# A four-layer residual LoRA kernel: the activation laid out batch by batch on chip, and one weight's split moved to GpSimd

## The chip, the core and the metric

The kernel runs on one core of a Trainium2 chip. The metric is device microseconds (us) of one execution; the kernel before takes 321.08 us (median of 3 runs, 320.62 to 321.49). TensorE (PE) multiplies, VectorE (DVE), ScalarE (ACT) and GpSimd (POOL) work element by element, and SyncE (SP) and ACT issue transfers, each on a queue of its own; the two queues are served by the same 16 DMA engines.

## The reference

`x` is [8 batches, 128 tokens, 512 features], fp32. Four residual layers follow each other, each with weights picked by one id per batch:

```
x = x + x @ w0[id0[b]].T                                  # layer 0: a whole 512x512 matrix per batch
x = x + x @ W.T + 2 * sum_e gate_e * (x @ A_e.T) @ B_e.T  # layer 1: router logits x @ Wr.T + 5*onehot(id1), top 2 of 8
x = x + x @ W.T + bias + 0.5 * (x @ A[id2[b]]) @ B.T      # layer 2
g, u = x@Wg.T + 0.5*lora_g, x@Wu.T + 0.5*lora_u           # layer 3, adapters by id3[b], inner size 1376
x = x + down(silu(g) * u) + 0.5*lora_d
```

## The kernel before, in words

The features lie on the 128 partitions in C = 4 chunks, and tokens run along the free dimension: `x_f` is a [128, 4, 1024] tile (chunk, then token; token = batch * 128 + position). Host code lays `x` out in DRAM as [batch][partition][chunk][token], so that one batch has 2 KB in a row per partition in DRAM.

The products want fp32 accuracy from a fast format (fp32r). So an operand is split into a high part (a copy that rounds to fp32r, `high`, on ACT, line 406) and a low part (the difference, `low`, on DVE, line 592), and a product is three matmuls: high x high, high x low, low x high. The activation of layer 0 is split on POOL instead (lines 390 and 392, batches 1 to 7, chunks 1 to 3, into `xa`).

**Layer 0** (lines 909 to 938) goes batch by batch. Batch 0 is four plain fp32 products, one for each chunk, straight from `x_f` and the landed weight (line 918, two records each). Batches 1 to 7 take chunk 0 in plain fp32 (line 921) and chunks 1 to 3 as split products (lines 929 to 931), each behind its weight's low part (`w0_lo`) and, from the second instruction on, behind `x0_lo`, the batch's own split on POOL. The tokens-major result goes to `y0` (ACT, line 418), is transposed back by PE (line 879) and added into `x_f` by DVE (line 605), which is then split into `xb` (ACT and DVE). From batch 3 on, PE also makes layer 1's thin product for one batch behind each layer-0 product (`thin1`, line 899, eight matmuls with `aw1_hl`, the LoRA A matrices and the router's weights side by side, 136 columns).

**What sets the order** is each engine's hand-written program and its semaphores; no planner.

- ACT's queue first issues all eight loads of `x` (line 427), one a batch, in order. Its first compute instruction stands behind them.
- SP's queue reads the ids, and then issues batch 0's weight in four pieces of 256 KB (`w0c_in`, line 306), batches 1 and 2 in three pieces each (line 315; 512, 256 and 256 KB), then `aw1` (272 KB, line 321), and, once PE is done with batch 0 (`l0_tm >= 1`), batch 3's. Batches 4 to 7 wait for the ring of three buffers (`w0_raw_used`, `w0_lo`).
- ACT splits each piece as it lands; at the start of b = 3 it first splits `aw1` (lines 432 and 433). DVE does the low parts in the same order, with `aw1`'s ahead of batch 3's (lines 642 and 643). PE waits for `aw1`'s low part after batch 3's product (line 936).

```
pool.wait_ge(x_in[b], 16)
pool.tensor_copy(xa[:, 0, 1:C, cols], x_f[:, 1:C, cols]).then_inc(x0_hi, 1)
```

Layers 1 to 3 then run over two halves of 512 tokens. The layer's sum is added into `x_f` by DVE (lines 707, 709 and 835), split again (lines 462 and 717), and the last sum is sent out in nine pieces by SP (line 375), each behind its add.

Of the kernel before, what the change touches and what calls it, by code (L numbers as in the profile page):

```python
# [28 lines left out]
F32 = mybir.dt.float32  # L29
# [3 lines left out]
ALU = mybir.AluOpType  # L33
# [4 lines left out]
B, S, D = 8, 128, 512  # L38
C = D // P
# [19 lines left out]
def bass_four_residual_layers(nc, xT, ids0, ids1, ids2, ids3, w0, w1, aw1, b1, w2, a2, b2, bias2,  # L59
                              wgu, agu, sel, bgu, wd, ad, bd, out):  # L60
    ctx = ExitStack()
    with ctx:
# [3 lines left out]
        def at(name, off, shape, dt=F32):  # L66
            return nc.alloc_sbuf_tensor_at(name, [P, *shape], dt, offset=base + off)
# [13 lines left out]
        o_misc = o_ad + 11 * KB  # L81


        x_f = at("x_f", o_xf, [C, T])
        xa = at("xa", o_xa, [2, C, T], F32R)
        xb = at("xb", o_xb, [2, C, T], F32R)

# [82 lines left out]
        def sem(name):  # L170
            return ctx.enter_context(nc.semaphore(name))
# [15 lines left out]
        const_step, ident_ready, masks_ready, iota_ready = (sem(n) for n in (  # L187
            "const_step", "ident_ready", "masks_ready", "iota_ready"))
        t3_zeroed, td_zeroed = sem("t3_zeroed"), sem("td_zeroed")
        x0_hi, x0_lo = sem("x0_hi"), sem("x0_lo")  # L190

        w0_raw_used, l0_tm, l0_tr = sem("w0_raw_used"), sem("l0_tm"), sem("l0_tr")
        l1_tm, l1_tr = sem("l1_tm"), sem("l1_tr")
# [34 lines left out]
            return bank[4 + j if h == 0 else j]  # L228


        splits = ["aw1"] + [f"w1_{o}" for o in range(C)] + ["b1", "a2"] + [f"w2_{o}" for o in range(C)] + ["b2", "agu"]
        nth = {name: i + 1 for i, name in enumerate(splits)}

        def split_views(name):

            if name == "aw1":
                return aw1_raw[:], aw1_hl[:, :, 0], aw1_hl[:, :, 1]
            if name == "b1":
                return b1_raw[:], b1_hl[:, 0], b1_hl[:, 1]
            if name == "a2":  # L240
                return a2_raw[:], a2_hl[:, :, :, 0], a2_hl[:, :, :, 1]
            if name == "agu":
                return agu_raw[:], agu_hl[:, :, :, 0], agu_hl[:, :, :, 1]
            if name == "b2":
                return b2_raw[:], b2_st[:], None
            raw, hl = (w1_raw, w1_hl) if name[1] == "1" else (w2_raw, w2_hl)
            o = int(name[3:])
            return raw[:, o], hl[:, 0, o], hl[:, 1, o]

        split_source = {"aw1": (aw1_in, 16), "b1": (b1_in, 16), "a2": (a2_in, 16 * B), "agu": (agu_in, 16 * B),  # L250
                        "b2": (b2_in, 16)}
        for o in range(C):
            split_source[f"w1_{o}"] = (w1_in[o], 16)
# [40 lines left out]
        def _(sp):  # L294
# [77 lines left out]
            sp.dma_start(wd_raw[3][:], wd[3]).then_inc(wd_in[3], 16)  # L372
            for i, (o, cols) in enumerate(DOWN_PIECES):
                sp.wait_ge(x3_sum, i + 1)
                sp.dma_start(out[o, :, cols], x_f[:, o, cols]).then_inc(out_sent, 16)
            sp.wait_ge(out_sent, 16 * len(DOWN_PIECES))


        @block.gpsimd
        def _(pool):  # L380
            pool.memset(ident[:], 0.0).then_inc(const_step, 1)
            pool.wait_ge(const_step, 1)
            pool.affine_select(out=ident[:], in_=ident[:], compare_op=ALU.not_equal, fill=1.0, base=0,
                               pattern=[[-1, P]], channel_multiplier=1).then_inc(ident_ready, 1)
            pool.iota(iota_e[:], [[1, E]], base=0, channel_multiplier=0,
                      allow_small_or_imprecise_dtypes=True).then_inc(iota_ready, 1)
            for b in range(1, B):
                cols = slice(b * S, (b + 1) * S)
                pool.wait_ge(x_in[b], 16)
                pool.tensor_copy(xa[:, 0, 1:C, cols], x_f[:, 1:C, cols]).then_inc(x0_hi, 1)  # L390
                pool.wait_ge(x0_hi, b)
                pool.tensor_tensor(xa[:, 1, 1:C, cols], x_f[:, 1:C, cols],
                                   xa[:, 0, 1:C, cols].bitcast(F32), ALU.subtract).then_inc(x0_lo, 1)
            pool.wait_ge(l0_tr, B)
            pool.wait_ge(w12_lo, nth["a2"])
            pool.memset(t3_st[:].bitcast(F32), 0.0).then_inc(t3_zeroed, 1)
            pool.wait_ge(sel_copied, 1)
            pool.wait_ge(hi_lo_copied, 1)
            pool.memset(td_st[:].bitcast(F32), 0.0).then_inc(td_zeroed, 1)
# [3 lines left out]
        def _(act):  # L403
# [16 lines left out]
            def x1_high(b):  # L420
                cols = slice(b * S, (b + 1) * S)
                act.wait_ge(x1_sum, b + 1)
                high(xb[:, 0, :, cols], x_f[:, :, cols]).then_inc(x1_hi, 1)


            for b in range(B):
                act.dma_start(x_f[:, :, b * S:(b + 1) * S], xT[b]).then_inc(x_in[b], 16)

            for b in range(1, B):
                if b > W0_RING:  # L430
                    act.wait_ge(l0_tm, b - W0_RING + 1)
                if b == 3:
                    split_hi("aw1")
                for k in range(KC):
                    if k == KC - 1:
                        copy_y0(b - 1)
                    act.wait_ge(w0_in[b % W0_RING][k], w0_landed(b))
                    high(w0_hl[b % W0_RING][:, 0, k], w0_raw[b % W0_RING][:, 1 + k]).then_inc(w0_hi, 1)
                if b == 7:
                    split_hi("w1_0")  # L440
                    split_hi("w1_1")
                if b >= 2:
                    x1_high(b - 2)
# [13 lines left out]

            def x_high(l, h, o):
                n = number(l, h, o)
                dst = (xa if l == 1 else xb)[:, 0, o, h * HT:(h + 1) * HT]  # L460
                act.wait_ge(x_sum, n + 1)
                high(dst, x_f[:, o, h * HT:(h + 1) * HT]).then_inc(x_hi, 1)


            router_exp(0)
# [123 lines left out]
        def _(dve):  # L589
# [10 lines left out]
                    low(lo, raw, hi).then_inc(w12_lo, 1)  # L600

            def x1_add(b):
                cols = slice(b * S, (b + 1) * S)
                dve.wait_ge(l0_tr, b + 1)
                dve.tensor_tensor(x_f[:, :, cols], bank[2 + b % 2][:].rearrange("p (c t) -> p c t", c=C),
                                  x_f[:, :, cols], ALU.add).then_inc(x1_sum, 1)

            def x1_low(b):
                cols = slice(b * S, (b + 1) * S)
                dve.wait_ge(x1_hi, b + 1)  # L610
                low(xb[:, 1, :, cols], x_f[:, :, cols], xb[:, 0, :, cols]).then_inc(x1_lo, 1)

            def sum_ranks1(h, j):

# [24 lines left out]
            last.then_inc(masks_ready, 1)  # L639

            for b in range(1, B):
                if b == 3:
                    split_lo("aw1")
                for k in range(KC):
                    dve.wait_ge(w0_hi, KC * (b - 1) + k + 1)
                    low(w0_hl[b % W0_RING][:, 1, k], w0_raw[b % W0_RING][:, 1 + k],
                        w0_hl[b % W0_RING][:, 0, k]).then_inc(w0_lo, 1)
                if b == 7:
                    split_lo("w1_0")
                    split_lo("w1_1")  # L650
                x1_add(b - 1)
                if b >= 2:
                    x1_low(b - 2)
                if b == 4:
                    bias_of_language()
                if b >= 5:
                    sum_ranks1(0, b - 5)
# [43 lines left out]

            def x_add(l, h, o):
                n = number(l, h, o)
                dst = x_f[:, o, h * HT:(h + 1) * HT]
                dve.wait_ge(main_done, n + 1)
                if l == 1:
                    ins = dve.tensor_tensor(dst, bank[4 + n % 4][:], dst, ALU.add)
                else:
                    ins = dve.scalar_tensor_tensor(out=dst, in0=bank[4 + n % 4][:], scalar=bias_sb[:, o:o + 1],  # L709
                                                   in1=dst, op0=ALU.add, op1=ALU.add)  # L710
                ins.then_inc(x_sum, 1)

            def x_low(l, h, o):
                cols = slice(h * HT, (h + 1) * HT)
                xs = xa if l == 1 else xb
                dve.wait_ge(x_hi, number(l, h, o) + 1)
                low(xs[:, 1, o, cols], x_f[:, o, cols], xs[:, 0, o, cols]).then_inc(x_lo, 1)


            router(0)  # L720
# [109 lines left out]

            def x3_add(i):
                o, cols = DOWN_PIECES[i]
                dst = x_f[:, o, cols]
                dve.wait_ge(down_done, i + 1)
                dve.tensor_tensor(dst, down_bank(o, cols), dst, ALU.add).then_inc(x3_sum, 1)  # L835

            t3_uv_low(0)
            t3_low(0)
# [37 lines left out]
        def _(pe):  # L876
# [32 lines left out]
            for b in range(B):  # L909
# [5 lines left out]
                if b == 0:  # L915
                    for c in range(C):
                        pe.wait_ge(w0c_in[c], 16)
                        ins = pe.matmul(bank[0][:], x_f[:, c, cols], raw[:, c], start=(c == 0), stop=(c == C - 1))  # L918
                else:
                    pe.wait_ge(w0_in[b % W0_RING][0], w0_landed(b))  # L920
                    pe.matmul(bank[b % 2][:], x_f[:, 0, cols], raw[:, 0], start=True,  # L921
                              stop=False).then_inc(w0_raw_used, 1)
                    pe.wait_ge(x0_lo, b)
                    hl = w0_hl[b % W0_RING]
# [8 lines left out]
                ins.then_inc(l0_tm, 1)  # L933

                if b == 3:
                    pe.wait_ge(w12_lo, nth["aw1"])
                if 3 <= b < 7:
                    thin1(0, b - 3)

# [266 lines left out]
```

## Time and profile before

| | us |
|---|---|
| median of 3 runs | 321.08 (320.62 to 321.49) |
| the profiled execution's own time | 321.29 |
| its span (first to last instruction) | 319.5 |
| PE busy in the span | 310.6 (97%) |
| DVE, ACT, POOL busy | 151.4, 107.4, 15.4 |
| HBM read, written | 30.89 MB, 2.10 MB |

Times in the trace count from the span's start. The profiled execution took 1.79 us more than its span. PE is busy nearly throughout; where it is not, and where its clock is granted at half, is in the first 30 us, and the rows further down are mostly of that stretch. A matmul's record can overlap its neighbours', since matmuls are pipelined, so lengths of stages are read from starts.

### The profile page before, as it was taken

The numbers are of one execution on the slowest core, as the hardware profiler recorded it, in microseconds if no ns is written. First come the engines' busy times: TensorE is split into PE (matmuls) and PEld (weight loads), VectorE is DVE, ScalarE is ACT, GpSimd is POOL, SyncE is SP. The second block draws the span as 40 slices with busy tenths as digits, with TensorE's granted clock in tenths as the row PEclk, the third lists the DMA queues.
The fourth block names the chain that finished last, engine by engine and source line by source line (L and its number), as shares of the span: only waits on it lengthen the run. The fifth ranks groups of instructions, "written<-read, shape, count | busy, mean of one in ns | idle before, by whom it ended". The sixth has DMA issues, their size and how long they took to land.

```text
span 319.5 us, 4612 instructions
## 1 busy us (share of the span) xinstructions
PE 310.6 (97%) x1672; PEld 257.0 (80%) x1672; DVE 151.4 (47%) x251; ACT 107.4 (34%) x165; POOL 15.4 (5%) x23
## 2 busy tenths in 40 slices
PE   5898999999999999999999999999999999999996
PEld 4366788888888888888888888888889788897886
DVE  0088897885769446364254254254624531011101
ACT  0277662513446247144144144145325220000000
POOL 2542000200100000000000000000000000000000
PEclk9599999999999999999999999999999999999999
DMA  5999982005203500422421421550642001000111
GB/s 132 364 330 312 373 266 71 0 0 171 94 0 101 157 10 0 130 78 58 131 78 54 131 84 47 148 163 0 173 140 90 2 0 66 35 33 2 55 44 35
DMA packets 24016, 33.21 MB, mean 104 GB/s; under 512 B 3264, under 2 KB 16320, under 8 KB 23872
## 3 DMA queue, kind: packets, MB, share of 16 engines
q1 hardware_dynamic: 19776, 30.90, 30.4%
q10 hardware_dynamic: 4224, 2.10, 2.3%
q8 instruction: 10, 0.16, 0.2%
q14 instruction: 6, 0.05, 0.1%
HBM read 30.89 MB, written 2.10 MB: 103 GB/s over the span
## 4 chain that ended last, share of the span: by engine, by line
PE 95%; DMA 2%; DVE 1%; SPq 1%; issue 0%
PE bank L945 24%; PE bank L946 24%; PE bank L947 24%; PE bank L1090 3%; PE bank L1046 3%; PE bank L899 3%; PE bank L992 2%; DMA w_raw<-in_w 2%; PE bank L921 2%; PE bank L918 2%; PE bank L929 2%; PE bank L931 1%; PE bank L930 1%; PE bank L879 1%; SPq L297 1%; PE bank L1113 1%
## 5 line engine op out<-in xcount | busy, mean ns | idle before, releaser
L945 PE MATMUL bank<-xb,wgu_hl 128*128 128x512 f32 x176 | 69.1, 392 | 0.0
L946 PE MATMUL bank<-xb,wgu_hl 128*128 128x512 f32 x176 | 69.0, 392 | 0.0
L947 PE MATMUL bank<-xb,wgu_hl 128*128 128x512 f32 x176 | 68.5, 389 | 0.0
L947 PEld LDWEIGHTS bank<-xb,wgu_hl 128*128 128x128 f32 x176 | 33.1, 188 | 7.2
L804 DVE TENSOR_TENSOR act_f<-bank,act_f 128x512 f32<-128x512 f32 x22 | 15.2, 691 | 48.2 <-PE bank L1046 46.4
L945 PEld LDWEIGHTS bank<-xb,wgu_hl 128*128 128x128 f32 x176 | 33.0, 188 | 5.8
L946 PEld LDWEIGHTS bank<-xb,wgu_hl 128*128 128x128 f32 x176 | 33.2, 189 | 5.3
L945 PE MATMUL bank<-act_hl,wd_hl 128*128 128x512 f32 (+1 forms) x99 | 36.6, 370 | 0.0
L946 PE MATMUL bank<-act_hl,wd_hl 128*128 128x512 f32 (+1 forms) x99 | 36.2, 366 | 0.0
L947 PE MATMUL bank<-act_hl,wd_hl 128*128 128x512 f32 (+1 forms) x99 | 36.2, 366 | 0.0
L406 ACT ACTIVATE act_hl<-act_f 128x512 f32 (+1 forms) x22 | 13.9, 632 | 61.7 <-DVE act_f L804 61.7
L592 DVE TENSOR_TENSOR w_hl<-w_raw,w_hl 128x512 fp32r<-128x512 f32 x29 | 20.1, 724 | 15.7 <-ACT w_hl L406 15.5
L592 DVE TENSOR_TENSOR act_hl<-act_f,act_hl 128x512 f32 (+1 forms) x22 | 15.2, 692 | 19.2 <-ACT act_hl L406 19.2
L835 DVE TENSOR_TENSOR x_f<-bank,x_f 128x512 f32<-128x512 f32 (+1 forms) x9 | 5.5, 630 | 37.6 <-PE bank L1113 37.6
L945 PEld LDWEIGHTS bank<-act_hl,wd_hl 128*128 128x128 f32 x99 | 18.7, 189 | 3.3 <-issue 0.5
L947 PEld LDWEIGHTS bank<-act_hl,wd_hl 128*128 128x128 f32 x99 | 18.7, 189 | 3.1
L946 PEld LDWEIGHTS bank<-act_hl,wd_hl 128*128 128x128 f32 x99 | 18.7, 189 | 2.8
L406 ACT ACTIVATE w_hl<-w_raw 128x512 fp32r<-128x512 f32 x29 | 17.7, 624 | 8.6 <-DMA w_raw<-in_w 8.6
L1046 PEld LDWEIGHTS bank<-t_st,bgu_st 128*128 128x128 f32 x88 | 16.1, 188 | 3.3 <-DVE t_st L796 0.2
L525 ACT ACTIVATE act_f<-bank 128x512 f32<-128x512 f32 x22 | 12.9, 588 | 15.7 <-PE bank L1046 15.7
L1046 PE MATMUL bank<-t_st,bgu_st 128*128 128x256 f32 x88 | 17.2, 282 | 0.0
L406 ACT ACTIVATE xb<-x_f 128x512 fp32r<-128x512 f32 x16 | 10.0, 628 | 16.9 <-DVE x_f L709 12.8
(127 smaller groups left out, 449.5 us busy)
## 6 DMA issues: line engine op xcount, KB each, us to landing
w_raw<-in_w SPq DMA_DIRECT2D x22, 256.0 KB, 7.0
wgu_raw<-in_wgu SPq DMA_DIRECT2D x11, 512.0 KB, 3.5
bgu_raw<-in_bgu SPq DMA_DIRECT2D x88, 64.0 KB, 2.2
w_raw<-in_w SPq DMA_DIRECT2D x7, 512.0 KB, 6.3
x_f<-in_xT ACTq DMA_DIRECT2D x8, 256.0 KB, 8.4
out<-x_f SPq DMA_DIRECT2D x7, 256.0 KB, 2.1
wd_own<-in_wd SPq DMA_DIRECT2D x2, 704.0 KB, 4.8
wd_raw<-in_wd SPq DMA_DIRECT2D x2, 704.0 KB, 4.4
```

Of the source, the lines that this page charges most:

```text
L406: return act.activation(dst, src, ACT.Copy)
L525: act.activation(act_f[h][:], bank[4 + 2 * h][:], ACT.Silu).then_inc(silu_done, 1)
L592: return dve.tensor_tensor(dst, src, hi.bitcast(F32), ALU.subtract)
L804: dve.tensor_tensor(act_f[h][:], bank[5 + 2 * h][:], act_f[h][:], ALU.mult).then_inc(act_mul, 1)
L899: ins = pe.matmul(thin1_bank(h, j)[:, 0:2 * TM1], xb[:, k, c, cols], aw1_hl[:, c].rearrange("p k n -> p (k n)"), start=(c == 0 and k == 0) ...
L918: ins = pe.matmul(bank[0][:], x_f[:, c, cols], raw[:, c], start=(c == 0), stop=(c == C - 1))
L921: pe.matmul(bank[b % 2][:], x_f[:, 0, cols], raw[:, 0], start=True, stop=False).then_inc(w0_raw_used, 1)
L945: pe.matmul(dst, w_hi, x[0][:, cols], start=start, stop=False)
L946: pe.matmul(dst, w_hi, x[1][:, cols], start=False, stop=False)
L947: return pe.matmul(dst, w_lo, x[0][:, cols], start=False, stop=stop)
L1046: ins = pe.matmul(bank[4 + 2 * h + g][:, q * 2 * S:(q + 1) * 2 * S], bgu_st[slot][:, pair, g], t3_st[:, g, pair * 2 * S:(pair + 1) * 2 * S ...
L1090: ins = pe.matmul(bank[h][0:2 * R, j * S:(j + 1) * S], ad_hl[:, b, f].rearrange("p k r -> p (k r)"), act_hl[:, f, k, b * S:(b + 1) * S], s ...
```

## The change

Three edits:

1. `x_f` becomes [128, 8 batches, 4 chunks, 128 tokens]. A batch's load now writes 2 KB in one run on each partition, where it wrote four runs of 512 B. All other uses are rewritten to the same elements: one batch becomes contiguous, and half a chunk (512 tokens) becomes four runs of 512 B, in the DVE adds, the splits and in the output's transfers.
2. `aw1`'s split leaves ACT and DVE and goes to POOL, behind the split of batch 2 of `x` and ahead of that of batch 3, and has a semaphore of its own (`aw1_split`), for which PE waits after batch 3's product.
3. `aw1` leaves the list of splits that ACT and DVE count through.

The order of the transfers on both queues stays: the eight loads of `x` still stand first on ACT's.

```diff
-        x_f = at("x_f", o_xf, [C, T])
+        x_f = at("x_f", o_xf, [B, C, S])
...
+        def by_batch(tokens):
+            return tokens.rearrange("p (b s) -> p b s", s=S)
+        def x_f_tokens(o, cols):
+            return x_f[:, cols.start // S:cols.stop // S, o]
...
-        splits = ["aw1"] + [f"w1_{o}" for o in range(C)] + ["b1", "a2"] + [f"w2_{o}" for o in range(C)] + ["b2", "agu"]
+        splits = [f"w1_{o}" for o in range(C)] + ["b1", "a2"] + [f"w2_{o}" for o in range(C)] + ["b2", "agu"]
...
-                sp.dma_start(out[o, :, cols], x_f[:, o, cols]).then_inc(out_sent, 16)
+                sp.dma_start(out[o, :, cols].rearrange("p (b s) -> p b s", s=S), x_f_tokens(o, cols)).then_inc(out_sent, 16)
...
-                pool.tensor_copy(xa[:, 0, 1:C, cols], x_f[:, 1:C, cols]).then_inc(x0_hi, 1)
+                pool.tensor_copy(xa[:, 0, 1:C, cols], x_f[:, b, 1:C]).then_inc(x0_hi, 1)
                 pool.wait_ge(x0_hi, b)
-                pool.tensor_tensor(xa[:, 1, 1:C, cols], x_f[:, 1:C, cols],
+                pool.tensor_tensor(xa[:, 1, 1:C, cols], x_f[:, b, 1:C],
                                    xa[:, 0, 1:C, cols].bitcast(F32), ALU.subtract).then_inc(x0_lo, 1)
+                if b == 2:
+                    pool.wait_ge(aw1_in, 16)
+                    pool.tensor_copy(aw1_hl[:, :, 0], aw1_raw[:]).then_inc(aw1_split, 1)
+                    pool.wait_ge(aw1_split, 1)
+                    pool.tensor_tensor(aw1_hl[:, :, 1], aw1_raw[:], aw1_hl[:, :, 0].bitcast(F32),
+                                       ALU.subtract).then_inc(aw1_split, 1)
...
-                act.dma_start(x_f[:, :, b * S:(b + 1) * S], xT[b]).then_inc(x_in[b], 16)
+                act.dma_start(x_f[:, b], xT[b]).then_inc(x_in[b], 16)
...
-                if b == 3:
-                    split_hi("aw1")
...
-                if b == 3:
-                    split_lo("aw1")
...
-                dst = x_f[:, o, cols]
+                dst = x_f_tokens(o, cols)
                 dve.wait_ge(down_done, i + 1)
-                dve.tensor_tensor(dst, down_bank(o, cols), dst, ALU.add).then_inc(x3_sum, 1)
+                dve.tensor_tensor(dst, by_batch(down_bank(o, cols)), dst, ALU.add).then_inc(x3_sum, 1)
...
                 if b == 3:
-                    pe.wait_ge(w12_lo, nth["aw1"])
+                    pe.wait_ge(aw1_split, 2)
```

## Rows read from the trace of the kernel before

**Rows 1.** The page's busy times: engine, busy us, share, instructions.

```profile
PE 310.6 (97%) x1672; PEld 257.0 (80%) x1672; DVE 151.4 (47%) x251; ACT 107.4 (34%) x165; POOL 15.4 (5%) x23
```

**Rows 2.** The chain of waits, 3 to 30 us: start, us, what.

```profile
3.69 7.61 DMA w_raw<-in_w
...
23.67 0.63 DVE aw_hl L592
24.30 0.92 DVE w_hl L592
```

**Rows 3.** Stretches: length, busy us (instructions) by engine, clock, DMA share, GB/s.

```profile
5.00:8.00 3.00, 0.74 (x4) 0.44 (x3) 0.00 (x0) 0.00 (x0) 1.49 (x2) 1.00 0.88 173
9.00:16.40 7.40, 7.11 (x9) 2.69 (x10) 0.69 (x1) 2.47 (x3) 4.43 (x6) 0.54 1.08 373
16.40:19.63 3.23, 3.23 (x16) 2.31 (x15) 2.58 (x4) 2.24 (x5) 2.02 (x2) 1.00 1.05 362
19.63:23.03 3.40, 3.40 (x16) 2.30 (x15) 2.73 (x5) 2.49 (x6) 1.78 (x2) 1.00 0.98 347
23.03:29.20 6.17, 4.94 (x24) 3.48 (x24) 6.17 (x9) 4.56 (x9) 2.07 (x3) 1.00 0.84 274
29.20:33.58 4.38, 4.38 (x25) 3.47 (x24) 3.20 (x8) 2.97 (x6) 0.00 (x0) 1.00 0.98 361
```

**Rows 4.** PE in order of time: start, us, instruction, [idle before <- what ended it].

```profile
9.05 2.04 PE L918 MATMUL bank<-w_raw,x_f 128*128 128x512 f32 x2 [3.31 <-DMA w_raw<-in_w]
11.34 5.06 PE L918 MATMUL bank<-w_raw,x_f 128*128 128x512 f32 x6 [0.24 <-DMA w_raw<-in_w]
25.36 0.47 PE L929 MATMUL bank<-w_hl,xa 128*128 128x512 f32 x1 [1.23 <-DVE w_hl L592]
```

**Rows 5.** Queues before w0's first packet, 2.4 to 5 us: packets, MB, share.

```profile
q10 hardware_dynamic: 1093, 0.54, 77.2%
```

**Rows 6.** Queues, 5 to 8 us (q10 is ACT's, q1 SP's).

```profile
q1 hardware_dynamic: 134, 0.25, 56.1%
q10 hardware_dynamic: 528, 0.27, 31.9%
```

**Rows 7.** Queues, 14 to 16 us.

```profile
q1 hardware_dynamic: 278, 0.60, 82.8%
q10 hardware_dynamic: 280, 0.14, 24.7%
```

**Rows 8.** Issues of lines 427, 306 and 321: ns each, first and last start.

```profile
L427 ACTq DMA_DIRECT2D x_f<-in_xT x8: 632/652/2796, 0.8 to 6.4; - x8
L306 SPq DMA_DIRECT2D w_raw<-in_w x4: 410/589/957, 3.1 to 5.2; - x4
L321 SPq DMA_DIRECT2D aw_raw<-in_aw x1: 424/424/424, 9.7 to 9.7; - x1
DMA to landing us min/median/max: 11.4/11.4/11.4
```

**Rows 9.** Instructions that touch x_f: ns min/median/max, first and last start, form.

```profile
L406 ACT ACTIVATE xb<-x_f x16: 618/632/636, 20.8 to 107.5; 128x512 fp32r<-128x512 f32 x16
L592 DVE TENSOR_TENSOR xb<-x_f,xb x16: 675/682/1239, 22.4 to 108.1; 128x512 fp32r<-128x512 f32 x16
...
L605 DVE TENSOR_TENSOR x_f<-bank,x_f x8: 676/690/692, 18.4 to 51.7; 128x512 f32<-128x512 f32 x8
L707 DVE TENSOR_TENSOR x_f<-bank,x_f x8: 682/688/692, 58.5 to 79.8; 128x512 f32<-128x512 f32 x8
...
L390 POOL CAST xa<-x_f x7: 502/503/864, 5.0 to 24.0; 128x384 fp32r<-128x384 f32 x7
L392 POOL TENSOR_TENSOR xa<-x_f,xa x7: 991/996/1512, 5.6 to 24.7; 128x384 fp32r<-128x384 f32 x7
```

**Rows 10.** POOL and DVE in order of time: start, us, instruction.

```profile
22.11 1.01 POOL L392 TENSOR_TENSOR xa<-x_f,xa 128x384 fp32r<-128x384 f32 x1
...
24.23 3.01 DVE L592 TENSOR_TENSOR w_hl<-w_raw,w_hl 128x512 fp32r<-128x512 f32 x3
```

More of the change, by code:

```diff
@@ L189, in bass_four_residual_layers @@
         t3_zeroed, td_zeroed = sem("t3_zeroed"), sem("td_zeroed")
-        x0_hi, x0_lo = sem("x0_hi"), sem("x0_lo")
+        x0_hi, x0_lo, aw1_split = sem("x0_hi"), sem("x0_lo"), sem("aw1_split")
         w0_raw_used, l0_tm, l0_tr = sem("w0_raw_used"), sem("l0_tm"), sem("l0_tr")
@@ L228, in thin1_bank @@
             return bank[4 + j if h == 0 else j]
-        splits = ["aw1"] + [f"w1_{o}" for o in range(C)] + ["b1", "a2"] + [f"w2_{o}" for o in range(C)] + ["b2", "agu"]
+        def by_batch(tokens):
[3 more added lines that the diff above has]
+        splits = [f"w1_{o}" for o in range(C)] + ["b1", "a2"] + [f"w2_{o}" for o in range(C)] + ["b2", "agu"]
         nth = {name: i + 1 for i, name in enumerate(splits)}
         def split_views(name):
-            if name == "aw1":
-                return aw1_raw[:], aw1_hl[:, :, 0], aw1_hl[:, :, 1]
             if name == "b1":
@@ L248, in split_views @@
             return raw[:, o], hl[:, 0, o], hl[:, 1, o]
-        split_source = {"aw1": (aw1_in, 16), "b1": (b1_in, 16), "a2": (a2_in, 16 * B), "agu": (agu_in, 16 * B),
+        split_source = {"b1": (b1_in, 16), "a2": (a2_in, 16 * B), "agu": (agu_in, 16 * B),
                         "b2": (b2_in, 16)}
@@ L422, in x1_high @@
                 act.wait_ge(x1_sum, b + 1)
-                high(xb[:, 0, :, cols], x_f[:, :, cols]).then_inc(x1_hi, 1)
+                high(xb[:, 0, :, cols], x_f[:, b]).then_inc(x1_hi, 1)
             for b in range(B):
-                act.dma_start(x_f[:, :, b * S:(b + 1) * S], xT[b]).then_inc(x_in[b], 16)
+                act.dma_start(x_f[:, b], xT[b]).then_inc(x_in[b], 16)
             for b in range(1, B):
@@ L459, in x_high @@
                 n = number(l, h, o)
-                dst = (xa if l == 1 else xb)[:, 0, o, h * HT:(h + 1) * HT]
+                cols = slice(h * HT, (h + 1) * HT)
+                dst = (xa if l == 1 else xb)[:, 0, o, cols]
                 act.wait_ge(x_sum, n + 1)
-                high(dst, x_f[:, o, h * HT:(h + 1) * HT]).then_inc(x_hi, 1)
+                high(by_batch(dst), x_f_tokens(o, cols)).then_inc(x_hi, 1)
             router_exp(0)
@@ L602, in x1_add @@
             def x1_add(b):
-                cols = slice(b * S, (b + 1) * S)
                 dve.wait_ge(l0_tr, b + 1)
-                dve.tensor_tensor(x_f[:, :, cols], bank[2 + b % 2][:].rearrange("p (c t) -> p c t", c=C),
-                                  x_f[:, :, cols], ALU.add).then_inc(x1_sum, 1)
+                dve.tensor_tensor(x_f[:, b], bank[2 + b % 2][:].rearrange("p (c t) -> p c t", c=C),
+                                  x_f[:, b], ALU.add).then_inc(x1_sum, 1)
             def x1_low(b):
@@ L610, in x1_low @@
                 dve.wait_ge(x1_hi, b + 1)
-                low(xb[:, 1, :, cols], x_f[:, :, cols], xb[:, 0, :, cols]).then_inc(x1_lo, 1)
+                low(xb[:, 1, :, cols], x_f[:, b], xb[:, 0, :, cols]).then_inc(x1_lo, 1)
             def sum_ranks1(h, j):
@@ L703, in x_add @@
                 n = number(l, h, o)
-                dst = x_f[:, o, h * HT:(h + 1) * HT]
+                dst = x_f_tokens(o, slice(h * HT, (h + 1) * HT))
                 dve.wait_ge(main_done, n + 1)
                 if l == 1:
-                    ins = dve.tensor_tensor(dst, bank[4 + n % 4][:], dst, ALU.add)
+                    ins = dve.tensor_tensor(dst, by_batch(bank[4 + n % 4][:]), dst, ALU.add)
                 else:
-                    ins = dve.scalar_tensor_tensor(out=dst, in0=bank[4 + n % 4][:], scalar=bias_sb[:, o:o + 1],
+                    ins = dve.scalar_tensor_tensor(out=dst, in0=by_batch(bank[4 + n % 4][:]), scalar=bias_sb[:, o:o + 1],
                                                    in1=dst, op0=ALU.add, op1=ALU.add)
@@ L716, in x_low @@
                 dve.wait_ge(x_hi, number(l, h, o) + 1)
-                low(xs[:, 1, o, cols], x_f[:, o, cols], xs[:, 0, o, cols]).then_inc(x_lo, 1)
+                low(by_batch(xs[:, 1, o, cols]), x_f_tokens(o, cols), by_batch(xs[:, 0, o, cols])).then_inc(x_lo, 1)
             router(0)
@@ L917, in _ @@
                         pe.wait_ge(w0c_in[c], 16)
-                        ins = pe.matmul(bank[0][:], x_f[:, c, cols], raw[:, c], start=(c == 0), stop=(c == C - 1))
+                        ins = pe.matmul(bank[0][:], x_f[:, b, c], raw[:, c], start=(c == 0), stop=(c == C - 1))
                 else:
                     pe.wait_ge(w0_in[b % W0_RING][0], w0_landed(b))
-                    pe.matmul(bank[b % 2][:], x_f[:, 0, cols], raw[:, 0], start=True,
+                    pe.matmul(bank[b % 2][:], x_f[:, b, 0], raw[:, 0], start=True,
                               stop=False).then_inc(w0_raw_used, 1)
```

## The prediction, as recorded before the run

> **What bounds the kernel now.** I read the page's busy times first, then the chain of waits, then the first 30 us by stretches. PE is busy 310.6 us of the 319.5 us span [rows 1], and the chain leaves PE only at the start and at the very end. So an edit pays only where PE waits or runs slowly, and that is in layer 0. Three things stand there. (1) The chain waits 7.61 us for a piece of batch 0's weight (3.69 to 11.30) [rows 2]; PE had been idle 3.31 us when its first product began at 9.05, and waited again until 11.34 [rows 4]. (2) From 9.0 to 16.4 the granted clock is 0.54, nearly all of it the 1.2 GHz level [rows 3], after that idle stretch: the four plain products take 1.7 us each (5.06 us for three) [rows 4]. (3) Batch 3's stretch, 23.03 to 29.20, takes 6.17 us where batch 4's, with the same instructions, takes 4.38: 1.79 us too much [rows 3], 1.23 us of it one wait for a low part of the weight [rows 4]; the chain shows `aw1`'s low part (0.63 us) just ahead of it [rows 2]. After 29.2 PE has no gap worth naming until the end.
>
> In between, batches 1 and 2 take 3.23 and 3.40 us with PE always busy [rows 3]. So the time is that at which PE starts batch 4 (29.20), plus a fixed rest, plus the tail. I work out the new time of that start.
>
> **Part 1: the loads of x in 2 KB runs.** ACT issues a batch of x (512 runs of 512 B) in 0.65 us, and its last issue takes 2.8 us; SP issues a piece of the same 256 KB in 2 KB runs in 0.41 us undisturbed, and in up to 0.96 while ACT issues [rows 8]. Up to 5.0 us only x moves, 1093 packets, 0.54 MB [rows 5]. From 5 to 8 us, where both queues have issued megabytes, only 173 GB/s pass [rows 3], against 373 in the next stage. In those 3 us SP's queue has 134 packets (1.9 KB on average) for 56% of the engines' time, 0.2 us each; from 14 to 16 us it has 278, mostly as large, in 83% of 2 us, 0.10 us each [rows 6, 7]. So the data paths are not full there: packets wait for something. I take that to be the supply of packets out of the two issue queues, since x's loads alone bring 4224 packets where 2 KB runs would bring some 1,150. What speaks against it is that w0's first pieces might be slow of themselves; it is a rival below.
>
> Forecast of the transfers, if the supply is what was missing: x flows at 365 GB/s (rates of 347 to 373 once both flow [rows 3]) from about 2.8 us, so 0.8 MB of its 2.1 MB is in by 5.0, where w0 joins. Then the queues take turns packet by packet: 278 against 280 from 14 to 16 us [rows 7]. Before, a turn gave x 512 B and w0 2 KB or 4 KB; now x gets 2 KB too, half of the rate. w0 runs at 182 GB/s: its four first pieces of 0.26 MB come every 1.44 us, at 6.8, 8.3, 9.7 and 11.2 us (0.4 us from last byte to semaphore, my allowance). Before, the first two came at 9.0 and 11.3 [rows 2, 4]. By 10.8 us x has 0.25 MB left; batch 1's weight (1.05 MB) is through at 10.8 + (0.25 + 1.05)/0.365 = 14.35, so 14.75 with the allowance. `aw1` comes after batch 2's weight: + (1.05 + 0.28)/0.365 = 3.6, so 18.4. Before it landed at 9.7 + 11.4 = 21.1 [rows 8].
>
> PE: batch 0 ends at 11.2 + 0.86 = 12.1 at 2.4 GHz, or 12.9 at 1.2 GHz (I can't tell which level; idle before it shrinks from 3.31 us to 1.1). Neither binds: batch 1 is bound by its last piece: 14.75, high part 0.63, low part 0.69 [rows 9], 0.3 of handing over, three matmuls of 0.23: 17.1, against 19.63. If the clock is low until 15.8 as before, I reckon 17.5. Batch 2: + 3.40 = 20.5 (its pieces are through at 17.6, their low parts by 19.0). Batch 3's weight is issued when batch 0 ends, lands behind `aw1` from 19.8 to 21.3, low parts from 21.2 to 22.7; its last three matmuls stand some 2.4 us into the stage, so it is just in time.
>
> Everything that touches x_f elsewhere changes shape only. DVE's add already writes x_f in four runs at line 605 (690 ns) and in one at line 707 (688 ns) [rows 9]: nothing. ACT's and DVE's splits of x_f (632 and 682 ns) likewise: nothing; below nothing is excluded by the same pair. TensorE reads 128 adjacent tokens as before. The sends of the output go to 512 B runs: 256 for the last piece where there were 128. By the issues of x (0.65 us for 512 runs, 0.41 for 128 [rows 8]) that is + 0.08, and perhaps + 0.07 in the transfer; I take + 0.15 us at the end, bounds 0 and 0.4. The other eight sends lie beside PE.
>
> **Part 2: `aw1` on POOL.** ACT loses one instruction of 0.65 us and DVE one of 0.71 (0.63 on the chain [rows 2]). POOL gets two of 544 elements: by its 384-element rows, 0.50 x 544/384 = 0.71 and 0.99 x 544/384 = 1.40 us [rows 9]. But POOL waits for `aw1`'s landing, and behind that wait stand the splits of x's batches 3 to 7, for which PE waits (`x0_lo`) behind its first two matmuls of a batch. With `aw1` in at 18.4: 0.71 + 1.40 + 0.50 + 0.99, and 0.3 between them, gives batch 3's split at 22.3, if nothing disturbs POOL. PE wants it at 20.5 + 0.86 = 21.4: a new wait of 0.9 us. So the wait of batch 3 [rows 4] does not go away: POOL takes DVE's place. Batches 4 to 7 follow at 1.6 us each, under PE's 4.38: no wait.
>
> POOL beside DVE: from 24 us DVE took 3.01 us for three low parts that alone take 3 x 0.68 = 2.05 [rows 9, 10], beside 2.07 us of POOL [rows 3], and POOL's own instructions reach 0.86 and 1.51 us where the median is 0.50 and 1.00 [rows 9]. Somebody loses some 0.5 us for each us side by side. On the 3.6 us before batch 3's split I charge 0.6 us (bounds 0, and 2.1 if all stretch by 1.6).
>
> The Trainium skill, "SBUF — State Buffer", section "Who interferes with whom", says that a DVE instruction with two SBUF inputs and a GpSimd instruction that reads SBUF exclude each other, and the later one blocks fully. The trace agrees where it can be seen: one low part of x took 1.24 us [rows 9], begun 0.3 us into a POOL instruction of 1.01 us [rows 10]. By that rule moving work from DVE to POOL frees nothing of DVE's time while POOL has a backlog; what it gives is a rival of its own below.
>
> **The sum.** Batch 3 ends at 20.5 + 4.38 + 0.9 + 0.6 = 26.4, against 29.20: 2.8 us sooner, less 0.15 for the tail: 2.65. The profiled execution took 321.29 us, its span 319.5 and 1.79 around it; the span becomes 316.85 and the time 318.6. The median of the runs shown is 0.2 lower (321.08); I leave the forecast at **318.6 us**.
>
> **The rivals.**
>
> A. *DVE becomes the bound* (the rule above as a mechanism). x being in early, POOL works without pause after `aw1`: 2.1 + 5 x 1.5 = 9.6 us from 18.4. From 18.4 DVE owes, up to batch 4's last low part, seven low parts of weights, two adds and two splits of x: 11 x 0.69 = 7.6 us, so 26.0. If it loses 0.46 us per us of POOL (0.96 of 2.07 in the rows above), 4.4 us more: 30.4. Batch 4's stretch then ends at 30.4 + 0.7 + 1.2 (its last matmuls and the thin product) = 32.3, against 33.58: 1.3 us gained, with the tail 1.15: 320.1. For: DVE's 6.17 of 6.17 us busy in batch 3's stretch [rows 3]. Against: some of the loss in the rows was POOL's.
>
> B. *The slow stretch from 5 to 8 us stays*, because w0's own first packets are slow. Then the bytes set all: `aw1`, before which the same bytes pass, lands at 21.1 again, batch 3's split on POOL comes at 21.1 + 3.9 + 0.6 = 25.6, against 25.36 for the wait that it replaces; PE then runs 3.5 us without the rest of the old waits: 29.1. With the tail: 321.3, no change. For: long packets on SP's queue alone [rows 6].
>
> C. *Slower: batch 3's split, queued behind `aw1`.* As B, with POOL losing each meeting with DVE, as its longest rows show: 1.2 + 2.1 + 0.86 + 1.5 + 0.3 = 6.0 us after 21.1: 27.1, and batch 4 starts at 30.6, 1.4 us late, with the tail 1.55: 322.8. It decides once `aw1` lands later than 25.36 - 6.0 = 19.4 us in this worst case, or 21.2 undisturbed. Equal turns for x could bring that about.
>
> **Chances.** Forecast 0.52, A 0.16, B 0.18, C 0.14. A measurement of this kernel can tell 0.3% (0.96 us) from no change: faster is below 320.1, slower above 322.0. Forecast and most of A are faster, with some of A and B on the line: faster 0.66, same 0.20, slower 0.14. The lower end is the forecast without POOL's wait and losses: 17.1 + 3.40 + 4.38 = 24.9, 4.3 us gained, 317.0, and 0.4 less if no allowance is due: 316.6. The upper end takes in A and B: 321.8. The forecast's own range is 316.6 to 320.0.
>
> **What would show it.** Right: over 300 GB/s from 5 to 8 us, ACT's eight issues done by 5 us instead of 9.2, PE's first product before 8 us, batch 1 ended near 17 and `aw1` landed near 18.5; in batch 3 PE waiting for POOL, not DVE; batch 4 started near 26.4. Wrong: a rate under 200 GB/s from 5 to 8 us (B or C); w0's first two pieces later than 9.0 and 11.3 (equal turns hurt); batch 4's start as forecast but batch 5's late (A); a last send more than 0.4 us longer. If the clock stayed at 1.2 GHz beyond batch 1, each later us at it would cost up to half a us, which I have not charged.

## The result, and the profile after

The changed kernel takes 322.37 us (median of 20 runs, 320.96 to 323.53) against 321.11 us before (20 runs): a ratio of 1.0036, 95% interval 1.0023 to 1.0048. A time of 318.6 us was forecast; it is slower by 0.36%. Its profiled execution took 322.60 us with a span of 320.8.

The loads of x did what the edit asks of them, on the page:

```profile
PE 309.8 (97%) x1672; PEld 256.2 (80%) x1672; DVE 154.1 (48%) x250; ACT 106.9 (33%) x164; POOL 19.8 (6%) x25
...
q10 hardware_dynamic: 1152, 2.10, 2.0%
```

ACT's queue has 1152 packets where it had 4224. DVE is busy 154.1 us, 2.7 us more than before [rows 1], with one instruction less: some of its work got slower. POOL is busy 4.4 us more, of which `aw1`'s two instructions explain half.

The stages of batches 1 to 5 after the change (the columns of [rows 3]; each begins with the batch's first product):

```profile
16.26:19.65 3.39, 3.39 (x17) 2.47 (x15) 2.84 (x5) 2.61 (x5) 0.00 (x0) 1.00 1.04 363
19.65:23.70 4.05, 3.65 (x16) 2.38 (x15) 3.40 (x5) 2.67 (x5) 3.70 (x4) 1.00 0.41 151
23.70:29.91 6.21, 5.05 (x24) 3.33 (x23) 6.21 (x7) 3.38 (x6) 5.98 (x6) 1.00 0.78 247
29.91:34.57 4.66, 4.66 (x26) 3.42 (x24) 4.59 (x8) 3.23 (x6) 3.58 (x3) 1.00 1.02 356
34.57:39.19 4.62, 4.62 (x26) 3.38 (x24) 4.24 (x9) 2.68 (x6) 0.00 (x0) 1.00 0.91 283
```

Against [rows 3], batch 2's stage begins when it did (19.65 for 19.63) and takes 4.05 us for 3.40; batch 3's keeps its excess (6.21 for 6.17); batch 4's takes 4.66 for 4.38 and batch 5's 4.62 for 4.39. These four add up to 1.2 us, and every later matmul starts 1.2 us later; the tail adds 0.1, as the sends of 512 B runs take 0.37 us to issue for 0.33 and land in 2.4 us (median) for 2.1. In each stage that is slower, POOL is busy beside DVE or DVE is still behind from it. DVE had lost time to POOL before too, some 2 us from 19 to 30 us, most of it in the instructions of 1.24 and 3.01 us of [rows 9, 10]; after the change it is some 5 us.

PE's first product starts 1.5 us later than in [rows 4], after 5.27 us of idling:

```profile
10.56 5.86 PE L927 MATMUL bank<-w_raw,x_f 128*128 128x512 f32 x8 [5.27 <-DMA w_raw<-in_w]
```

### The profile page after: what moved, and what is told of

It reads as the page before. It is cut to its first block, busy times and chain, and to the rows that moved or that the text cites. A ratio compares the mean times of both kernels' runs of the same rounds, so it can differ in the third digit from the quotient of the medians.

```text
span 320.8 us, 4612 instructions
## 1 busy us (share of the span) xinstructions
PE 309.8 (97%) x1672; PEld 256.2 (80%) x1672; DVE 154.1 (48%) x250; ACT 106.9 (33%) x164; POOL 19.8 (6%) x25
## 3 DMA queue, kind: packets, MB, share of 16 engines
q10 hardware_dynamic: 1152, 2.10, 2.0%
## 4 chain that ended last, share of the span: by engine, by line
PE 94%; DMA 2%; DVE 2%; SPq 1%; ACT 0%; issue 0%
PE bank L954 24%; PE bank L955 24%; PE bank L956 24%; PE bank L1099 3%; PE bank L1055 3%; PE bank L908 3%; PE bank L1001 2%; DMA w_raw<-in_w 2%; PE bank L927 2%; PE bank L938 2%; PE bank L930 1%; PE bank L940 1%; PE bank L939 1%; PE bank L888 1%; DVE w_hl L604 1%; SPq L304 1%
## 5 line engine op out<-in xcount | busy, mean ns | idle before, releaser
L419 ACT ACTIVATE act_hl<-act_f 128x512 f32 (+1 forms) x22 | 13.9, 633 | 61.7 <-DVE act_f L813 61.7
L604 DVE TENSOR_TENSOR w_hl<-w_raw,w_hl 128x512 fp32r<-128x512 f32 x29 | 22.8, 824 | 15.8 <-ACT w_hl L419 15.8
L419 ACT ACTIVATE w_hl<-w_raw 128x512 fp32r<-128x512 f32 x29 | 17.6, 624 | 12.3 <-DMA w_raw<-in_w 12.1
```

Source lines behind the costliest of these rows:

```text
L419: return act.activation(dst, src, ACT.Copy)
L604: return dve.tensor_tensor(dst, src, hi.bitcast(F32), ALU.subtract)
```

## The experiments

Each kernel was timed beside the kernel before, and its ratio is to that. A kernel's own executions spread by 0.2 to 3.5 us, and a profile is of one of them. `layout_only`, the base of several, is the change without its POOL part. For the experiments, "theory P" is: the loss is POOL's. "Theory L": the loads'.

**1. The halves of the change, alone.** `layout_only`:

```diff
-                if b == 2:
-                    pool.wait_ge(aw1_in, 16)
-                    ... (POOL's split of aw1)
+        splits = ["aw1"] + ...          # and its split on ACT and DVE at b == 3, as before
```

> The changed kernel with aw1's split back on ACT and DVE, so only the layout of x_f and the 2 KB runs of its loads are left of the change. Theory P (the loss is POOL's: aw1's split and, queued behind it, five splits of x run beside DVE's, and each stretches the other): PE starts batch 3 near 23.05 as before, batch 4 at 28.4 to 29.2, DVE's three low parts of a batch take 2.1 us again instead of 3.3; time 320.3 to 321.2. Theory L (the loss is the loads': w0's first piece lands 1.5 us later because x takes equal turns): batch 4 starts near 29.9 as in the changed kernel, time 322.0 to 322.6.

Measured: 320.38 us, ratio 0.9986 (0.9967 to 1.0005). Theory L falls: the layout and the 2 KB runs cost nothing, and may bring 0.1%, which is not clear of noise. Batch 4 starts at 27.04 us in its profile, against 29.91, but that profile is of its fastest execution (319.34 of 319.34 to 322.54 us). It shows what early loads of x can bring: POOL is through with its splits at 14.8 us, no low part of DVE is slowed from then on, and batch 3's stage takes 5.08 us for 6.17.

`pool_only`, the kernel before with the POOL edit alone:

```diff
+                if b == 2:
+                    pool.wait_ge(aw1_in, 16)
+                    ... (POOL's split of aw1; ACT's and DVE's taken out)
```

> The kernel before (512 B runs, old layout) with aw1's split alone moved to POOL, behind batch 2's split of x. Theory P: aw1 lands at 21.1 as before, batch 3's split on POOL ends near 25.5, and POOL's backlog lies beside DVE to beyond 33 us; batch 4 starts at 29.9 or later, time 322.3 to 323.2, slower than the kernel before by the whole of the change's loss or more. Theory L: no loss from POOL, 320.6 to 321.4.

Measured: 323.57 us, ratio 1.0071 (1.0051 to 1.0090), batch 4 at 30.20. So the POOL edit alone loses twice what the whole change does, a little more than the range of theory P, which holds. Here, with `aw1` landed at 21.1 us, PE did wait for POOL, as the forecast had it, and for longer:

```profile
26.58 0.50 PE L929 MATMUL bank<-w_hl,xa 128*128 128x512 f32 x1 [2.65 <-POOL xa L390]
```

**2. The same work at another place in POOL's order.** `pool_last`:

```diff
-                if b == 2:
+                if b == 7:
                     pool.wait_ge(aw1_in, 16)
```

> The changed kernel with POOL's split of aw1 behind the split of batch 7 of x instead of behind batch 2's. All of x has landed by 12.8 us there, so POOL is through with x at about 14.3 us, before DVE's first low part at 15.8; only aw1's two instructions (about 2.4 us from 19.8) are left beside DVE. Theory P: the backlog's cost goes; batch 3 still starts 0.5 us late (aw1's own two instructions beside DVE), batches 4 to 7 at 4.4 us each: 320.2 to 321.2, at or under the kernel before. Theory L: 322.0 to 322.6 as the changed kernel.

Measured: 320.27 us, ratio 0.9982 (0.9963 to 1.0001). One constant is changed, and 2.1 us are gone (1.7 by the ratios). POOL's last split of x ends at 14.9 us, before DVE's first low part begins.

**3. The wait without the work.** `wait_only` is `layout_only` with POOL's wait alone:

```diff
+                if b == 2:
+                    pool.wait_ge(aw1_in, 16)
```

> layout_only (aw1 split by ACT and DVE), but POOL still waits for aw1's landing between its splits of batches 2 and 3 of x, without doing anything with it. Tells apart the two parts of what the change gave POOL: the two instructions on aw1, and the wait that holds back five splits of x until DVE is busy. Theory P1 (the held-back splits beside DVE are the cost): DVE's low parts from 20 to 30 us take 0.9 to 1.1 us each instead of 0.69, and the time is 321.2 to 322.4. Theory P2 (the two instructions are the cost): 320.2 to 320.8, as layout_only (320.4).

Measured: 322.86 us, ratio 1.0054 (1.0035 to 1.0073). Adding nothing but a wait to an engine that is busy 4% of the time in `layout_only` costs 2.5 us against it (2.2 by the ratios). P1 holds, with more loss than its range (322.4 at most, low parts of 1.1 us; they took 1.27): what costs is the time at which the five splits of x run. It isn't PE waiting for them either: batch 3's split was done at 21.4 us, and PE waited 2.61 us for DVE. DVE in order of time, first `layout_only`, where POOL is idle by then:

```profile
21.38 0.68 DVE L602 TENSOR_TENSOR xb<-x_f,xb 128x512 fp32r<-128x512 f32 x1
21.97 0.72 DVE L602 TENSOR_TENSOR aw_hl<-aw_raw,aw_hl 128x544 fp32r<-128x544 f32 x1
22.61 1.89 DVE L602 TENSOR_TENSOR w_hl<-w_raw,w_hl 128x512 fp32r<-128x512 f32 x3
24.84 0.69 DVE L614 TENSOR_TENSOR x_f<-bank,x_f 128x512 f32<-128x512 f32 x1 [0.35 <-PE bank L888]
```

and `wait_only`:

```profile
22.46 1.48 DVE L604 TENSOR_TENSOR xb<-x_f,xb 128x512 fp32r<-128x512 f32 x1
23.86 1.02 DVE L604 TENSOR_TENSOR aw_hl<-aw_raw,aw_hl 128x544 fp32r<-128x544 f32 x1
24.80 3.81 DVE L604 TENSOR_TENSOR w_hl<-w_raw,w_hl 128x512 fp32r<-128x512 f32 x3
28.53 0.68 DVE L616 TENSOR_TENSOR x_f<-bank,x_f 128x512 f32<-128x512 f32 x1
```

Same instructions, same shapes: the splits' low parts go from 0.68 to 1.48 and three of them from 1.89 to 3.81 us. The add that takes one input from a PSUM bank keeps its 0.68.

**4. What the loads do.** `x_behind_w0` gives w0's start to SP's queue alone:

```diff
             for b in range(B):
+                if b == 1:
+                    act.wait_ge(w0c_in[0], 16)
                 act.dma_start(x_f[:, b], xT[b]).then_inc(x_in[b], 16)
```

> layout_only, and ACT issues batch 0 of x, waits for the landing of the first piece of batch 0's weight, and issues batches 1 to 7 of x then. Asks what the 0.2 to 0.26 us packets of w0's start are. If they come from sharing with x, the first piece lands by 6.5 us and all four by 8.5, at over 300 GB/s; if w0's first packets are slow of themselves, the rate stays under 200 GB/s for some 2 us and the first piece lands near 7.5. Either way PE's first product starts 1.5 us or more before 9.05; batch 0 ends at 11.5 to 13.5 instead of 16.4, and as batch 3's weight is issued at that point, batch 4 starts at 26 to 28: 317.5 to 320. If something else bounds batches 1 to 3 (DVE, w0's bytes behind x), 320 to 321.

Measured: 324.11 us, ratio 1.0108 (1.0086 to 1.0130), slower than any case named. Batch 0 did go as hoped: first product at 6.33 us, all at the 2.4 GHz level, ended at 11.5 for 16.4. But batch 1 of x, issued at 6.2, landed at 14.25, eight microseconds later, behind w0's pieces that SP had issued meanwhile; from 5 to 10 us ACT's queue moved no packet at all:

```profile
14.29 1.57 PE L932 MATMUL bank<-w_raw,x_f 128*128 128x512 f32 x2 [2.75 <-DMA x_f<-in_xT]
```

PE idled for 2.75 us, its granted clock was 0.68 in the next stage, and all of POOL's splits of x, from 14.3 us on, ran beside DVE: batch 3's stage took 7.57 us.

`one_queue` puts both streams on SP's queue:

```diff
                 sp.dma_start(w0_raw[0][:, c], w0[adapter0[0]][:, c * D:(c + 1) * D]).then_inc(w0c_in[c], 16)
+            for b in range(1, B):
+                sp.dma_start(x_f[:, b], xT[b]).then_inc(x_in[b], 16)
...
-            for b in range(B):
-                act.dma_start(x_f[:, b], xT[b]).then_inc(x_in[b], 16)
+            act.dma_start(x_f[:, 0], xT[0]).then_inc(x_in[0], 16)
```

> layout_only (aw1 on ACT and DVE), but ACT issues only batch 0 of x, and SP issues batches 1 to 7 of x on its own queue behind batch 0's weight and ahead of batch 1's. Asks what makes packets slow (0.2 to 0.3 us each) where both queues have loads issued, from 5 to 8 us before and from 6.5 to 9 after the change. Theory Q (the issues of two queues get in each other's way, and what is issued later on one waits for what is issued on the other): with one queue no slow stretch, over 330 GB/s from 5.5 us on, batch 0's weight landed by 6.2, 7.2, 8.0 and 8.8 us, x complete by 14, batch 1's weight by 16.5, the third stage's start 1 to 2 us sooner than layout_only's: 318 to 320. Theory W (w0's first packets are slow of themselves): a slow stretch of 2 to 3 us again, batch 0's weight landed from 7 to 11 us, 320 to 322.

Measured: 322.16 us, ratio 1.0035 (1.0021 to 1.0048). Theory Q is right on the packets and wrong on the time. Packets of the queues, first the changed kernel from 6.5 to 9 us:

```profile
q10 hardware_dynamic: 148, 0.26, 33.7%
...
q1 hardware_dynamic: 125, 0.25, 65.6%
```

then `one_queue` from 5 to 8 us:

```profile
q1 hardware_dynamic: 420, 0.77, 82.7%
```

Share x stretch x 16 engines / packets gives 0.21 us for a 2 KB packet of w0 in the changed kernel and 0.095 in `one_queue`. The packets of x on ACT's queue took 0.09 us in the same stretch of the changed kernel, so only SP's were slow. Batch 0's weight was in by 9.6 us there, for 13.9 after the change. But 258 GB/s from 5 to 8 us is not the 330 that theory Q had, batch 1's weight then came only behind all of x, at 15.6 us, PE waited 3.68 us for it (granted clock 0.69 in the next stage), and POOL's later splits lay beside DVE. Bringing one stream forward pushed the other back.

**5. The clock.** `before_warm`, `layout_warm`, `after_warm` and `pool_last_warm` have one line changed:

```diff
-WARM_UP = 9
+WARM_UP = 27
```

> layout_only with 27 warm-up matmuls in place of 9, so that PE works until about 9.4 us and its first product finds it busy just before. Theory C (part of the loss of either kernel, and of the spread between executions, is batch 0 at the 1.2 GHz level after PE's idle stretch): the granted clock stays at the 2.4 GHz level from its rise on, batch 0's four products take 0.86 us each and end at about 14.0 (0.9 us after their last piece), batch 1's stretch is then bound by its own weight's landing: 1.0 to 2.0 us off: 318.4 to 319.4, and a smaller spread. Rival: batch 0 is bound by its pieces and what follows by batch 1's to 3's, so nothing comes of it: 320.2 to 320.8.

Measured: 319.18 us, ratio 0.9937 (0.9920 to 0.9955), all five runs within 319.10 to 319.29: the lowest median here. Batch 0's stage after the change, in `layout_only` and in `layout_warm`:

```profile
10.56:16.26 5.70, 5.70 (x8) 2.22 (x9) 0.42 (x1) 1.04 (x2) 0.00 (x0) 0.62 1.05 406
```

```profile
9.74:14.80 5.06, 5.06 (x8) 2.01 (x9) 0.00 (x0) 0.37 (x1) 4.82 (x7) 0.70 1.05 407
```

```profile
10.39:13.85 3.46, 3.46 (x10) 1.32 (x9) 0.00 (x0) 0.11 (x1) 3.30 (x6) 1.00 1.04 410
```

The granted clock is 1.00 instead of 0.62 and 0.70, and four products take 3.46 us instead of 5.70 and 5.06. Against `layout_only`'s profile, its fastest execution, that leaves little: batch 1 then waits 0.9 us for its weight's low part, batch 4 starts at 26.91 us for 27.04, and the two profiled times are 319.11 and 319.34. The 1.2 us between the medians come from `layout_only`'s other executions, and no profile shows what those lose. That the warm-ups make the spread small isn't shown either: `ids_early`, with the same warm-ups, spreads from 318.77 to 321.05.

> The kernel before with 27 warm-up matmuls in place of 9, nothing else. Theory C: batch 0 ends at 14.3 instead of 16.4 us (its last piece lands at 13.4), batch 1 at 18.6 to 19.0 instead of 19.6; batch 3's low parts are still late, so 0.3 to 1.0 us off: 320.1 to 320.8. Rival: no change, 321.2, since batch 3 is bound by its weight (landed 22.9 to 24.3), which is issued when batch 0 ends, and by DVE beside POOL.

Measured: 321.01 us, ratio 0.9998 (0.9986 to 1.0010): nothing, the rival of that expectation. Batch 1's products begin at 15.1 instead of 16.2, but batch 4 starts at 29.57 (29.20 before). Batch 1's stage is longer (4.44 us), with waits for its weight and the weight's low part, and so is batch 3's (6.44 us), where PE waits 1.82 us for DVE beside POOL.

> The changed kernel with 27 warm-up matmuls in place of 9, nothing else. Against layout_warm (319.2) it differs by POOL's block alone, now with the clock at its upper level in both. Theory P: POOL's backlog behind aw1 costs 2.0 us or more whatever the clock did: 321.2 to 321.8, a little under the changed kernel's 322.4. Rival (the clock was a good part of the change's loss): 319.5 to 320.5.

Measured: 321.11 us, ratio 0.9994 (0.9983 to 1.0006), just under theory P's range. Against `layout_warm` POOL's block costs 1.9 us with the clock at its upper level throughout, against 2.0 without. The same edit takes 1.3 us off the changed kernel (322.37 to 321.11; profiled 322.60 to 321.10, with batch 0's stage at 4.45 us for 5.70), so it pays there although DVE is the next bound: only with the old loads it brought nothing. In this trace PE waited for POOL's split of x, and after that for DVE in batch 5's stage, which took 5.52 us:

```profile
24.18 0.50 PE L938 MATMUL bank<-w_hl,xa 128*128 128x512 f32 x1 [1.34 <-POOL xa L399]
34.11 0.47 PE L938 MATMUL bank<-w_hl,xa 128*128 128x512 f32 x1 [0.90 <-DVE w_hl L604]
```

> pool_last with 27 warm-up matmuls. POOL's split of aw1 stands behind all of x's. Theory P says that what is left of its cost is one stretched low part in batch 2, paid for by the 0.7 us that DVE no longer spends on aw1: as layout_warm, 318.9 to 319.6. Rival: freeing ACT and DVE of aw1 is worth its 0.7 us: 318.4 to 318.8.

Measured: 319.49 us, ratio 0.9946 (0.9927 to 0.9964), as `layout_warm`: taking `aw1` off ACT and DVE shows no gain even where it stands well. In `pool_last`'s trace the two instructions stretch DVE's low parts of batch 2 (three in 3.42 us for 1.9), more than the 0.7 us that DVE saves; in this one only a split of x (1.01 us for 0.68), and batch 3's stage takes 4.79 us for 5.07. That 0.3 us is not seen in the times, and the loads of w0 came at other times in the two executions, so where it went stays open.

**6. The ids read earlier.** `ids_early` is `layout_warm` with

```diff
-                if b == W0_RING:
-                    adapter2 = ids_of(ids2, a2.shape[0] - 1)
-                    adapter3 = ids_of(ids3, agu.shape[0] - 1)
                 if b == 2:
...
+                    adapter2 = ids_of(ids2, a2.shape[0] - 1)
+                    adapter3 = ids_of(ids3, agu.shape[0] - 1)
```

> layout_warm, and SP's reading of the ids of layers 2 and 3 moves from behind batch 3's issues to behind aw1's, where SP waits for batch 0 anyway. In layout_warm SP issues batch 3's weight at 14.2 us and batch 4's only some 7 us later, though its buffer is free before. If batch 4's and later weights then land sooner and anything waits for them: 0.2 to 0.8 us off, 318.4 to 319.0. If PE's own work or DVE's bounds those batches: 319.2, no change.

Measured: 319.65 us, ratio 0.9948 (0.9931 to 0.9965): no gain over `layout_warm`. Batch 4's weight was issued at 18.35 us instead of 20.30, but PE waits for none of those weights.

## Why the prediction was wrong

**The reading of what bounds the kernel was right**: all of the change's 1.2 us arise before batch 6, and the rest is a constant. The profiled execution took 322.60 us where the sum gave 318.64. Of these 4.0 us, 2.5 are the late start of batch 2's stage (19.65 for 17.1), 0.65 its length (4.05 for 3.40), 0.3 batch 3's stage (6.21 us for 5.88, its stall included) and 0.5 those of batches 4 and 5. The first is the transfers' step, the others are POOL's.

**The transfers' step failed, by 3.6 us on its first number.** I had "w0 joins" at 5.0 us and its pieces at 6.8, 8.3, 9.7 and 11.2. That x would have 0.8 MB in by 5.0 was right:

```profile
q10 hardware_dynamic: 450, 0.83, 100.5%
```

But w0's first packet came at 6.5 us, 3.2 us after its issue (1.9 before), the slow packets followed as before (0.21 us each), and the pieces landed at 10.4, 12.3, 13.2 and 13.9. The reason I gave for the slow stretch, the many small packets of x, is refuted: a quarter of the packets, and it stayed. With only one queue loading it goes away, so w0's first packets are not slow of themselves, as rival B had it. Two queues in flight are not enough for it either: from 14 to 16 us before the change both moved packets, and SP's took 0.10 us [rows 7]. It is seen where SP's stream starts while x's is in flight. I took "packets wait for something" for "packets wait for the thing that this change removes". So batch 0 ended at 16.3, not 12.1, and batch 2's stage began at 19.65, not 17.1: 2.5 us of the forecast gain never arose. `layout_only` measures the edit of the loads at 0.8 us by the medians of its rounds and 0.45 by its ratio, within noise of nothing.

**POOL's step failed in its size, and in the sentence "Batches 4 to 7 follow at 1.6 us each, under PE's 4.38: no wait".** I looked at who waits for POOL, and priced the meeting with DVE for batch 3's split alone, at 0.6 us. In the profile of the changed kernel PE never waited for POOL; at 25.88, as before, it waited for DVE:

```profile
25.88 0.47 PE L938 MATMUL bank<-w_hl,xa 128*128 128x512 f32 x1 [1.16 <-DVE w_hl L604]
```

The stall that was forecast (0.9 us for POOL, + 0.6) exists: it was 1.34 us in `after_warm` and 2.65 in `pool_only`. In the changed kernel it was hidden, as PE came to batch 3 at 23.70 instead of 20.5 and DVE was later still. The chain of the changed kernel shows DVE's part:

```profile
21.00 1.84 DVE w_hl L604
22.83 0.60 DVE x_f L616
23.43 1.39 DVE xb L604
24.82 0.92 DVE w_hl L604
```

and POOL beside it:

```profile
19.84 1.01 POOL L403 CAST aw_hl<-aw_raw 128x544 fp32r<-128x544 f32 x1 [12.57 <-DMA aw_raw<-in_aw]
20.93 1.35 POOL L405 TENSOR_TENSOR aw_hl<-aw_raw,aw_hl 128x544 fp32r<-128x544 f32 x1
22.23 0.97 POOL L397 CAST xa<-x_f 128x384 fp32r<-128x384 f32 x1
23.28 1.00 POOL L399 TENSOR_TENSOR xa<-x_f,xa 128x384 fp32r<-128x384 f32 x1
```

From 20.9 to 33 us DVE's instructions with both inputs in SBUF took some 5 us more than alone. POOL's casts went from 0.50 to 0.97 us, so its backlog lasted 13.8 us, not 9.6. The cost of the block is 1.6 to 2.0 us (`after` against `layout_only`, with and without the low clock), where the sum took batch 3's excess of 1.79 us off and put a stall of 1.5 in its place.

**Rival A had the mechanism of POOL's part.** It put DVE's loss at 4.4 us; about 5 were measured. It had batch 4's stage end at 32.3; it ended at 34.57, 2.3 us late, about as much as batch 2's stage began late. That the one comes of the other is my reading; no run separates them. Its sign, batch 4's start as forecast and batch 5's late, was not seen in the changed kernel, where DVE already held up batches 2 and 3; a DVE wait in batch 5's stage shows in `after_warm`. I gave it 0.16, because I read "some of the loss in the rows was POOL's" as a reason for a smaller loss; a POOL that is slowed stays beside DVE for longer. The rule of the Trainium skill that I cited ("SBUF — State Buffer", "Who interferes with whom") agrees with the rows shown here: instructions of DVE with two SBUF inputs took up to 1.84 us beside POOL, the add with one PSUM input 0.68 throughout.

**Right**: the shapes of x_f cost nothing (DVE's adds 0.68 to 0.69 us), the tail + 0.1 us (0.15 forecast), ACT's issues done at 4.7 us for 9.2, `aw1` landed earlier, at 19.8 for 21.1.

What stays open: what x's stream does to the start of w0's that makes a packet take 0.2 us; and how much of the spread between executions (w0's first piece landed from 9.6 to 10.4 us in four profiles of kernels with the new loads, at 8.5 and 9.0 with the old) comes from it.

## What to carry to other kernels

An engine's place in its own order can cost more than its work: before a wait is put into a nearly idle engine, list what stands behind it, when that would have run, and which engine it will then run beside. Where POOL and DVE both work from SBUF, move work between them only if the one is idle when it lands, and price the meeting over the whole backlog. When a profile shows transfers waiting, test the cause (one queue, other order) before pricing its removal; and where PE idles ahead of its first products, a few more warm-up matmuls are cheap: here 0.6% against the kernel before, together with the layout, 0.4% on the changed kernel, and nothing on the kernel before alone.

## What the runs showed of the hardware

- With loads issued on both queues, a 2 KB packet of the stream that started second took 0.21 us for some 2.5 us, one of the first stream 0.09; with all but x's first load on one queue 0.095 us. Later, with both streams running, they were not slow (0.10 us from 14 to 16 us before the change).
- A load issued on one queue while the other had some 2 MB issued or being issued landed 8 us later (batch 1 of x in `x_behind_w0`, 6.2 to 14.25). The other way round, w0's first packet came 3.2 us after its issue behind 2 KB packets of x, 1.9 us behind 512 B ones.
- In a stretch where DVE and POOL both work from SBUF, both lose: DVE's three low parts 3.81 us for 1.89, POOL's cast 0.97 for 0.50. DVE's add with one PSUM input kept its 0.68.
- After 5.27 us of idling PE's first four products ran at a granted clock of 0.62 (5.70 us); with matmuls until they began, at 1.00 (3.46 us).
